# Bias rows folded into weight matrices, 112-column keys and scores, and re-spaced side work in a four-layer attention kernel

## What is computed

```
x = L0(x, ctx)                        # short attention to 32 chosen keys, 8 heads, out projection + b_out, + x
x = self_attn(LN(x)) + x              # L1: 20 heads of 64, output bias bo1
x = cross_attn(LN(x), ctx) + x        # L1: 20 heads, 1500 keys, output bias bo2
x = geglu(LN(x)) + x                  # L1: biases b_ff1, b_ff2
x = L2(x, ctx)                        # 8 heads, 1496 keys, plus a small branch, b_out
x = self_attn, cross_attn, geglu      # L3: 20 heads of 8; biases o1_b, o2_b, ff_b2
```

## Time and profile before

| | |
|---|---|
| median of 3 runs | 6159.2 us |
| the profiled execution, its own time | 6158.75 us |
| its span, first to last instruction | 6156.9 us |
| TensorE busy (matmul) | 5728.1 us |
| TensorE busy (weight load) | 4613.2 us |
| VectorE / ScalarE / GpSimd busy | 2843.0 / 3105.5 / 3112.4 us |
| mean granted TensorE clock | 0.958 |

### The profile page before, as it was taken

One profiled execution on the slowest core, in us unless ns is written; L12 is line 12 of the kernel. 1 busy time (PEld: TensorE's weight loads), 2 busy tenths in 40 slices (PEclk: granted clock), 3 DMA queues, 4 the chain that ended last, 5 costly groups with the idle time before them and its releaser, 6 DMA issues.

```text
span 6156.9 us, 92602 instructions
## 1 busy us (share of the span) xinstructions
PE 5728.1 (93%) x34384; PEld 4613.2 (75%) x34384; DVE 2843.0 (46%) x5170; ACT 3105.5 (50%) x7280; POOL 3112.4 (51%) x3472
## 2 busy tenths in 40 slices
PE   7999999999999999998999998899999999999998
PEld 5777777777777777776666666677777777777776
DVE  2444444444444444443555554344445554444452
ACT  1445554444554444453555454255555555555554
POOL 0444444444444444453555555155556555555564
PEclk9899999999999999997999999599999999999999
DMA  2000000000000000000111011000000000000000
GB/s 55 12 16 16 16 13 15 16 15 16 16 12 13 12 15 16 16 20 17 29 29 29 24 33 37 8 18 15 18 15 20 18 19 15 16 16 17 15 19 10
DMA packets 84429, 114.48 MB, mean 19 GB/s; under 512 B 42814, under 2 KB 64682, under 8 KB 83978
## 3 DMA queue, kind: packets, MB, share of 16 engines
q1 hardware_dynamic: 83978, 108.56, 6.2%
HBM read 104.06 MB, written 4.46 MB: 18 GB/s over the span
## 4 chain that ended last, share of the span: by engine, by line
PE 59%; DVE 13%; issue 11%; POOL 10%; ACT 4%; DMA 3%; POOLq 0%; SPq 0%; DVEq 0%; ACTq 0%
PE ps_c L687 11%; POOL p_lo L1606 9%; PE ps_c L1068 6%; PE ps_u L1141 5%; PE ps_s L1126 4%; PE ps_u L1143 4%; PE ps_u L1142 4%; PE ps_s L1128 4%; PE ps_s L1127 4%; DVE mpiece L1450 4%; PE ps_c L1087 3%; DMA w_area<-recs 1%; DVE uT L1477 1%; PE ps_c L893 1%; PE ps_c L867 1%
## 5 line engine op out<-in xcount | busy, mean ns | idle before, releaser
L1606 POOL TENSOR_TENSOR p_lo<-p,p_hi 125x448 fp32r<-125x448 f32 (+2 forms) x2688 | 2709.9, 1018 | 2257.6 <-ACT p_hi L1819 2163.1
L1817 ACT ACTIVATE p<-ps_s 125x448 f32<-125x448 f32 (+2 forms) x2688 | 1326.8, 494 | 2125.8 <-PE ps_s L1128 2023.6
L1819 ACT ACTIVATE p_hi<-ps_s 125x448 fp32r<-125x448 f32 (+2 forms) x2688 | 1318.6, 491 | 0.0
L1450 DVE TENSOR_REDUCE mpiece<-ps_c 125x1 f32<-125x500 f32 (+1 forms) x1984 | 1235.7, 669 | 123.9 <-PE ps_c L1068 116.8
L1141 PE MATMUL ps_u<-p_hi,ctx_hi 125*97 125x448 f32 (+2 forms) x2688 | 997.3, 371 | 103.2 <-POOL p_lo L1606 93.8
L1126 PE MATMUL ps_s<-q_hi,ctxT_hi 105*125 105x448 f32 (+3 forms) x2688 | 992.7, 369 | 22.6 <-DVE q_hi L1460 17.6
L1068 PE MATMUL ps_c<-ctxT_hi,q_hi 96*125 96x500 f32 (+1 forms) x2112 | 863.8, 431 | 87.7 <-DVE mpiece L1450 70.8
L1127 PE MATMUL ps_s<-q_lo,ctxT_hi 96*125 96x448 f32 (+2 forms) x2688 | 928.5, 345 | 0.0
L1128 PE MATMUL ps_s<-q_hi,ctxT_lo 96*125 96x448 f32 (+2 forms) x2688 | 926.0, 344 | 0.0
L1143 PE MATMUL ps_u<-p_lo,ctx_hi 125*97 125x448 f32 (+2 forms) x2688 | 918.3, 342 | 0.0
L1142 PE MATMUL ps_u<-p_hi,ctx_lo 125*96 125x448 f32 (+2 forms) x2688 | 917.4, 341 | 0.0
(11 more groups left out here) (231 smaller groups left out, 6006.1 us busy)
## 6 DMA issues: line engine op xcount, KB each, us to landing
ctx_raw<-in_ctx SPq DMA_DIRECT2D x96, 562.5 KB
pT<-recs SPq DMA_DIRECT2D x32, 420.0 KB, 3.3
w_area<-recs SPq DMA_DIRECT2D x32, 420.0 KB, 3.3
w_area<-recs SPq DMA_DIRECT2D x32, 168.0 KB, 3.2
cs<-in_ctx SPq DMA_DIRECT2D x192, 6.0 KB, 2.9
x_between<-x_out SPq DMA_DIRECT2D x32, 80.0 KB
x_in<-x_between SPq DMA_DIRECT2D x32, 80.0 KB
w_area<-in_L_xattn_wq SPq DMA_DIRECT2D x2, 800.0 KB, 5.8
```

What stands on the lines that cost most here:

```text
L1450: z = V.tensor_reduce(mpiece[0:wide, k, r:r + 1], C(0, wide, n % banks(t), 0, PIECE), AX.X, ALU.max)
L1606: P.tensor_tensor(p_lo[0:kp, k % 3, 0:w], p32[0:kp, k % 2, 0:w], p_hi[0:kp, k % 3, 0:w].bitcast(F32), ALU.subtract).then_inc(*sig("pl_ready"))
L1817: A(p32[0:kp, k % 2, 0:w], ps_s[0:kp, k % 2, 0:w], ACT.Exp, scale=DH[t.ph] ** -0.5)
L1819: A(p_hi[0:kp, k % 3, 0:w], ps_s[0:kp, k % 2, 0:w], ACT.Exp, scale=DH[t.ph] ** -0.5)\
```

## The change

1. **Bias rows.** Five of eight bias rows are loaded under the weights they belong to. `w_n`, `l0_wout` and `l3_o` get one more partition. `xT` gets a row of ones (one more VectorE memset at the start), and the attended rows' own sum row of `uT`, now normalised too, is the row of ones for `w_n`. The K = 1 matmuls of `project` and of `post` step 1 are gone; one matmul in each place has 81 or 97 partitions instead of 80 or 96. The biases of L1's self attention (L899) and of the two feed-forward products (L1106) stay.
2. **112 columns.** The projection of the keys in `pre_0`, the scores of `pre_0` (L867) and of `pre_2` (L999) leave out the padding of each 64-token block, and so do the two copies of the keys.
3. **Four slots apart.** In phases 0 and 2 the three multiplications of `uT` stand at positions 15, 19 and 23. With that, the look-ahead `pre` of a following phase starts at position 26 instead of 20.
4. **More room in six places** of `PARTS`.

```diff
@@ PARTS
-            "pre": ((40, 3, {4: 1, 7: 0.5, 8: 3, 10: 1, 14: 1.5, 16: 3, 18: 2, 22: 2, 27: 2, 30: 1, 34: 1, 35: 0.5, 37: 1,
-                             38: 1.5, 39: 2, 40: 4.5}), (29, 3.5, {5: 2, 15: 1.5, 22: 0.5, 23: 2}), (20, 2.5, {2: 3, 6: 1.5, 7: 0.5, 9: 2, 11: 0.5, 15: 1, 19: 2, 20: 1})),
+            "pre": ((40, 3, {4: 1, 7: 0.5, 8: 3, 10: 1.5, 14: 1.5, 16: 3, 18: 2, 22: 2, 27: 2.5, 30: 1.5, 34: 1, 35: 0.5, 37: 1,
+                             38: 1.5, 39: 2, 40: 4.5}), (29, 3.5, {5: 2, 15: 1.5, 22: 0.5, 23: 2}), (20, 2.5, {2: 3, 6: 1.5, 7: 0.5, 9: 2, 11: 0.5, 13: 1, 15: 1, 19: 2, 20: 1})),
-            "post": ((15, 3, {6: 1, 14: 1}), (2, 1.5, {}), (15, 3, {6: 1.5})),
+            "post": ((15, 3, {1: 1, 6: 1, 14: 1}), (2, 1.5, {}), (15, 3, {1: 0.5, 6: 1.5})),
...
-                    lanes = [lane([part("pre", side.pre, At(t.ph + 1, 0, ahead=True))], POST + 4.0)]
+                    lanes = [lane([part("pre", side.pre, At(t.ph + 1, 0, ahead=True))], POST + 10.0)]
@@ project
-                    mm(r, ones[DC:DC + 1, :], rows[t.ph][:, D * bias:D * bias + D], start=True, stop=False)
-                    both(r, lambda i: xT[:, i, :, :], lambda i: w[:, i, :], first=False).then_inc(*sig("rm_psum"))
+                    both(r, lambda i: xT[0:HF + i, i, :, :], lambda i: w[0:HF + i, i, :]).then_inc(*sig("rm_psum"))
@@ pre_0, projections and scores
-                            z = both(C(0, 128, 0, 128 * j, 128), lambda i: l1_w[w][:, i, 128 * j:128 * j + 128],
-                                     lambda i: hT[:, i, :, :])
+                            each = slice(0, T if w else S)
+                            z = both(C(0, 128, 0, 128 * j, 128).rearrange("p (b s) -> p b s", b=2)[:, :, each],
+                                     lambda i: l1_w[w][:, i, 128 * j:128 * j + 128], lambda i: hT[:, i, :, each])
...
-                            z = mm(C(S * b, S, 0, 128 * j, 128), qo3[:, j, S * b:S * b + S],
-                                   kb1[:, b, 2 * j:2 * j + 2, :], start=True, stop=True)
+                            z = mm(C(S * b, S, 0, 128 * j, 128).rearrange("p (e s) -> p e s", e=2)[:, :, 0:T],
+                                   qo3[:, j, S * b:S * b + S], kb1[:, b, 2 * j:2 * j + 2, 0:T], start=True, stop=True)
@@ post
-                    if t.ph != 1:
-                        mm(r, ones[DC:DC + 1, :], rows[t.ph][:, D * (2 - t.ph // 2):D * (3 - t.ph // 2)], start=True, stop=False)
                     for h in range(t.heads):
-                        z = mm(r, uT[0:DC, h, :, :], w_n[:, h, :], start=(t.ph == 1 and h == 0), stop=(h == t.heads - 1))
+                        k = DC + (t.ph != 1 and h == 0)
+                        z = mm(r, uT[0:k, h, :, :], w_n[0:k, h, :], start=(h == 0), stop=(h == t.heads - 1))
@@ normalise (VectorE)
-                        yield POST - 1 + g
+                        yield POST - 1 + (1 if t.ph == 1 else 4) * g
...
-                        u = uT[0:DC, h0:h0 + n, b, 0:T]
+                        u = uT[0:DC + 1, h0:h0 + n, b, 0:T]
```

More of the change, by code:

```diff
@@ L325, in other_loads @@
         def other_loads(ph):
-            r = [(rows[ph][:, D * i:D * i + D], a[n].rearrange("(o n) -> o n", o=1)) for i, n in enumerate(BIAS[ph])]
+            places = {"L1_xattn_bo2": w_n[DC:DC + 1, 0, :], "L3_xattn_o2_b": w_n[DC:DC + 1, 0, :],
+                      "L0_xattn_b_out": w_s[HF:HF + 1, 480:640], "L2_xattn_b_out": w_s[HF:HF + 1, 480:640],
+                      "L3_xattn_o1_b": w_o[HF:HF + 1, 1120:1280]}
+            r = [(places[n] if n in places else rows[ph][:, D * i:D * i + D], a[n].rearrange("(o n) -> o n", o=1))
+                 for i, n in enumerate(BIAS[ph])]
             for i, (g, b) in enumerate(LN[ph]):
@@ L776, in project @@
                 @staticmethod
-                def project(t, m, w, bias, bank):
+                def project(t, m, w, bank):
                     pe.wait_ge(*got("ot_ready", t, m + 1))
                     r = side_banks(t)(0, 128, bank, 0, D)
-                    mm(r, ones[DC:DC + 1, :], rows[t.ph][:, D * bias:D * bias + D], start=True, stop=False)
-                    both(r, lambda i: xT[:, i, :, :], lambda i: w[:, i, :], first=False).then_inc(*sig("rm_psum"))
+                    both(r, lambda i: xT[0:HF + i, i, :, :], lambda i: w[0:HF + i, i, :]).then_inc(*sig("rm_psum"))
                 @staticmethod
@@ L846, in pre_0 @@
                     yield 14
-                    side.project(t, 0, l0_wout, 0, 2)
+                    side.project(t, 0, l0_wout, 2)
                     yield 16
@@ L973, in pre_1 @@
                     yield 28
-                    side.project(t, 1, l0_wout, 0, 1)
+                    side.project(t, 1, l0_wout, 1)
                 @staticmethod
@@ L998, in pre_2 @@
                         for o, h0, h1 in ((0, 0, 8), (0, 8, 10), (1, 0, 6), (1, 6, 10)):
-                            z = mm(C(S * b, S, 0, 640 * o + S * h0, S * (h1 - h0)), q_small[:, o, b, :],
-                                   kb3[:, o, b, h0:h1, :], start=True, stop=True)
+                            z = mm(C(S * b, S, 0, 640 * o + S * h0, S * (h1 - h0)).rearrange("p (h s) -> p h s", s=S)[:, :, 0:T],
+                                   q_small[:, o, b, :], kb3[:, o, b, h0:h1, 0:T], start=True, stop=True)
                     z.then_inc(*sig("s_psum"))
@@ L1008, in pre_2 @@
                     yield 17
-                    side.project(t, 0, l3_o, 0, 2)
+                    side.project(t, 0, l3_o, 2)
                     yield 19
@@ L1172, in prologue @@
                         V.memset(q_hi[0:DC, :, 20 * T:].bitcast(F32), 0.0).then_inc(consts, 1)
+                        V.memset(xT[64:HF + 1, :, :, :], 1.0).then_inc(consts, 1)
                     dh, n0 = DH[ph], products_before(ph)
@@ L1668, in pre @@
                         act.wait_ge(*got("ot_psum", t, 1))
-                        A(xT[:, :, :, :], side_banks(t)(0, HF, 1, 0, 256).rearrange(two, a=2, b=2), ACT.Copy)\
+                        A(xT[0:HF, :, :, :], side_banks(t)(0, HF, 1, 0, 256).rearrange(two, a=2, b=2), ACT.Copy)\
                             .then_inc(*sig("ot_ready"))
@@ L1706, in pre @@
                         act.wait_ge(*got("ot_psum", t, 1))
-                        A(xT[:, :, :, :], side_banks(t)(0, HF, 0, 0, 256).rearrange(two, a=2, b=2), ACT.Copy)\
+                        A(xT[0:HF, :, :, :], side_banks(t)(0, HF, 0, 0, 256).rearrange(two, a=2, b=2), ACT.Copy)\
                             .then_inc(*sig("ot_ready"))
```

36 lines of the change are left out of this document (18 added, 18 removed).

## The result

The changed kernel takes 7170.4 us (median of 4 runs, 7155.9 to 7184.3), against 6157.9 us for the kernel before on the same chip: ratio 1.1637, 95% interval 1.1607 to 1.1668, some 1010 us slower. The prediction was 6083 us, faster. Its sign is wrong, and the time lies far outside its range. One execution of a later experiment, e11_before_space, took 16075.8 us at a mean granted clock of 0.78 against 0.961 to 0.964 in the others, and is left out of that experiment's median and ratio.

A forecast was written before the change was run, and what follows sets the result against it. TensorE's stream was taken to set the pace. Gains 36.8 + 17 + 1 + 3 + 21.4 + 5, less 2.5 (look-ahead) and 6 (`p_lo`), gave 75.7 us: 6159 to 6083 us, range 6040 to 6135.

The forecast's parts named there:

- The wider contraction: Matmuls at 81 and 97 partitions, with `uT`'s multiplication and broadcast one partition larger: no added column, costed at nothing.
- engines that are half idle: Claim that the extra partition in `uT`'s multiplication and broadcast would be paid on engines with idle time; no cost.
- The rival for "slower": Phase 0, second half: ScalarE's pT copy waits for `uT`'s third multiplication at position 23, delaying exponentials and TensorE; 6195 us; chance 0.03.
- outside the sum: TensorE's granted clock, left out of the terms: 0.005 in its mean is some 15 us either way.
- Key projection: `pre_0` key projection at 112 columns: the 128-column weight load sets the rhythm; 1 us gain, bounds 1 and 8.8.
- 112 columns in all: Padding left out of scores (17 us), key projection (1 us) and key copies (3 us).
- The six places: More room in `PARTS`: waits shortened at `post` step 1 and in `pre_0` and `pre_2`; 21.4 us, bounds 0 and 33.
- Four waits: TensorE's waits on `q_hi` (10.3 us), L1686 (7.2), L1733 (7.2) and L1666 (8.6), which the room was to shorten.
- the `sm` wait: `pre_0` step 10: wait moves from L764 to L755, on VectorE's `sm`, 6 to 10 us; net gain 1 us.
- What comes back at `p_lo`: Part of the savings returns as TensorE's waits on GpSimd's `p_lo`: 6 us taken off the gain.
- Bias: 80 bias matmuls of `project` and `post` removed at 0.46 us each: 36.8 us gain, bounds 22 and 44.
- Four slots apart: Spaced `uT` multiplications: no gain in phase 0, 5 us of `mpiece` waits in phase 2; bounds 0 and 20.

The follow-up runs named there:

- e11_before_space: Kernel before, with only the three `uT` multiplications four slots apart and the later look-ahead start: 6118.0 us, ratio 0.9925.
- e1: Kernel before, with only the broadcast of the reciprocals lengthened from 96 to 97 partitions, multiplication still reading 96: 7267.8 us, ratio 1.1793.
- e3: Changed kernel, with the broadcast as one transfer to 112 partitions: 6029.6 us, ratio 0.9777 to the kernel before.
- e4: Changed kernel, with the broadcast split into two transfers, 96 rows and one row: 6012.4 us, ratio 0.9749 to the kernel before.
- e7: Changed kernel with the broadcast as 96 + 1 rows, and key projection, scores and key copies back at 128 columns: 6025.2 us, ratio 0.9787 to the kernel before.
- e10: Kernel before, with only the more room in six places of `PARTS`: 6146.2 us, ratio 0.9964.
- e12: Kernel before, with only the bias rows, broadcast as 96 + 1 partitions: 6082.8 us, ratio 0.9876.

## Why the prediction was wrong

**The step that failed.** "The wider contraction (81 and 97 partitions) adds no column and no instruction; I cost it at nothing. `uT`'s multiplication and the broadcast get one partition more, again no column." For the matmuls and the multiplication that holds (0.62 us at 97 partitions). For the broadcast it is false by a factor: the prediction counted one row more and put it at nothing, where the time went by what the row count divides by. In phases 0 and 2 3.3 us became some 18 us, 64 times; in phase 1, where a row is 1792 bytes, the multiplication came 9 to 10 us after the issue, 32 times. The cover that the prediction named, "engines that are half idle", did not apply: the multiplication stands in VectorE's queue between reductions that TensorE needs within a few us. Those waits of TensorE grew by 492 (`mpiece`), 188 (`oz`), 127 (`kvb`) and 120 us (`uT`), 927 together; e1, with 896 us more on the same four, shows that they need nothing else of the change. The rival for "slower" looked at VectorE being late too, but for another reason (the third multiplication) and at 0.03; e3 and e4, with that spacing in place, rule it out.

**Why the range did not hold it.** No bound was set for the broadcast, since no row showed one of 97 rows. The slack of the transfer could be read: 3.3 us to land, and the multiplication 4.5 us after the issue in one half and 10.4 us in the other (1428.18 to 1438.55). Asking what a transfer late by ten us would do would have shown several hundred us at once. The repaired kernels, at 6030 and 6012 us, fall below the range as well; there, by the estimate above, it is mostly the clock, which stood outside the sum.

**What was right.**
- Key projection: 20 records with 112 moving columns still take as long as with 128. By form of the changed kernel, first 128 and then 112 columns moving: the same 0.13 us of busy time a record (82.2 and 81.9 us for 640).

```profile
L691 PE MATMUL ps_c<-hT,w_area 80*128 80x128 f32 x640 | 82.2, 287 | 0.9 <-ACT hT L1640 0.9
L691 PE MATMUL ps_c<-hT,w_area 80*128 80x112 f32 x640 | 81.9, 286 | 7.3 <-ACT qo L1679 7.3
```

- 112 columns in all: 17 + 1 + 3 = 21 us predicted, 23 us measured (e7), uncertain by 16 us, so this is agreement and no more.
- The six places: 21.4 us predicted, 22 us alone (e10). Four waits went as said, and `sm` at 9.1 us came in their place; the growth on `mpiece`, 17 us alone, was not in the sum, so the match of the total is in part luck. The waits of e4; `q_hi` at `post` (10.3 us in the earlier trace rows) and the copies at L687 and L764 (7.2 and 7.2 us) are not among them, with 1.3 us or less left of each:

```profile
PE ps_u L1145 <- POOL p_lo L1611: 94.8, 227, 1.2
PE ps_c L1073 <- DVE mpiece L1455: 77.0, 107, 2.5
...
PE ps_c L1078 <- DVE mneg L1460: 11.3, 17, 1.2
PE ps_c L760 <- DVE sm L1238: 9.1, 15, 3.5
```

  3.5 us of the `sm` wait were there before (once), so 5.6 us are new, for 7.8 us less at L764 (8.6 to 0.8): 2.2 us net, priced at 1.

**What was mis-sized.** *What comes back at `p_lo`*: 94.8 us in e4 against 93.8, 1 us and not the 6 us that I took off. *Bias*: 36.8 us priced; each removed matmul gives 0.46 to 0.49 us, as the rows said and not the 0.275 us of the mere stream, so the price of the matmul stands. The whole part measures 76 us. What is above 37 fits the clock only in part: in e12's profiled execution, 58 us shorter than that of before, TensorE's busy time fell by 55 us, 18 more than the price of the matmuls, and the rest was not followed. In phase 0 the short pairs save 8 x 1.65 = 13 us, but the dip in the stretch ahead of them stays. *Four slots apart*: 5 us priced, 46 alone and 52 undone. The term had the right place (waits on `mpiece`: 70.8 to 63.2 us in e11, 7.6 us) and left out the clock: e11's mean rose from 0.958 to 0.961 in the profiled execution, and is 0.963 to 0.964 in the four others. The prediction kept the clock outside the sum as "some 15 us either way" for 0.005 in its mean; it rose by 0.015 in e4 and fell by 0.073 in the changed kernel, and by its own last sentence that was a way to be wrong.

**What stays open.** What sets off a dip of the clock, and so where the gains of the spacing and of the room come from beyond their waits. The room is worth 22 us alone and 40 us as the last part, and the four parts 191 us for 155; neither difference is clear of noise. Neither is it settled whether two transfers are better than one of 112 rows: 17 us between e4 and e3, with overlapping intervals.

## What to carry to other kernels

When a tile grows by a partition, look at every DMA that fills it, and factor the new row count: 97 rows moved at the rate of one engine where 96 reached 16 times as much; here splitting off the odd row (96 + 1) and rounding up to 112 = 7 x 16 both mended it. An engine that is half idle is no cover for a wait in the middle of its queue: ask what stands behind the waiting instruction and how soon it is wanted. And where the mean granted clock is under 1 in a steady stretch, compare equal stretches pair by pair: here such dips cost about 1.6 us each, a change of a few slots in another engine's work made them come or go, and e11's gain of 46 us is a multiple of the 9 us of idle time that it took off TensorE. How many there are could not be told from the length of the waits.

## What the runs showed that was not expected

- One row more in a broadcast of 96 rows of 4480 bytes: landing in 3.3 us at up to 456 GB/s becomes some 18 us at 28 GB/s. 104 and 112 rows carry more bytes and stay close to 96 (with 104 rows VectorE waits 114 us in all against 81; 112 rows land in 3.6 us).
- Equal work on TensorE takes 60.17 or 61.8 us in the same program, by the granted clock alone (1.00 or 0.97); removing two matmuls of 0.49 us a pair, or moving two VectorE instructions by a few slots, or the room in the six places, made all or nearly all the pairs of the short kind. The same wait of 1.1 us stood ahead of stretches with a dip and without.
- After a wait of 15 us TensorE's 448-column matmuls run at 0.37 us instead of 0.21 us for some 6 us. Such stretches come on top of the waits, as e1 shows: 892 us more of idle time on TensorE and 215 us more of busy time for the same records.
